# Perceiver layer on one core: context rows stationary in the weighted sum, the softmax division moved to the outputs, the context's scale folded into the key weights

## The chip, the cores and the metric

One core of a Trainium2 chip runs the whole program. The metric is the device time of one execution in microseconds. An execution has a profile, whose span runs from the first to the last instruction.

## The reference, cut to what matters

The layer is a cross attention, then a causal linear attention, then a two-of-eight expert layer, each added to its input. The change lies in the cross attention: 16 batches, 64 latents and 1024 context rows each, 16 heads of 64, all float32.

```python
lat = layer_norm(latents, ln_lat_g, ln_lat_b)
ctx = layer_norm(context, ln_ctx_g, ln_ctx_b)
q = (lat @ Wq)                      # 16 heads x 64
k, v = jnp.split(ctx @ Wkv, 2, axis=-1)
k = apply_rope(k, cos, sin)         # [x1*cos - x2*sin, x2*cos + x1*sin]
attn = jnp.clip(einsum('bhnd,bhsd->bhns', q, k) * scale, -11.0, 11.0)
attn = jax.nn.softmax(attn, axis=-1)
out = einsum('bhns,bhsd->bhnd', attn, v)
return out @ Wo + bo
```

The kernel never forms v: it takes the weighted sum of the normalised context rows first and multiplies by the value weights afterwards.

## The kernel before, in words

The order of the work is written out by hand. Each engine has a list of instructions and waits on counting semaphores. The cross attention has 128 steps (16 batches x 8 pairs of heads); in each, every engine runs its own function `step(j)`.

Float32 data that TensorE shall take in one pass is split in a high part, rounded to the fast format, and a low part, the rest; a product is then three matmuls (high x high, high x low, low x high).

In step j of the kernel before, in the order of their engine's list:

- TensorE (`step`, from L1321): the scores of pair j, 64 instructions on 64x64 corners of the array (L1332); the keys of pair j+2, twelve matmuls of 512 columns (L1346); two transposes of a normalised context tile (L1353); two transposes of the divided sum (L1362); the weighted sum of pair j-1, 24 matmuls that load the softmax weights and move 256 or 258 columns of context (L1380 to L1382); the value projection of pair j-2, 16 instructions on 64x64 corners (L1392).
- VectorE (`step`, from L912): centring of a context tile (L857), the output's sum (L844), the clamp of the exponentials (`clamped`, L863), scale and shift of the tile (L869), its moments (L877, L890), the keys times sine and cosine (L884, L895), the low part of the transposed tile (L902), and as the last large item the low part of the softmax weights (`weights_low`, L910); then the reciprocal of the denominators (L940), one element per partition.
- ScalarE (`step`, from L613): the exponential (L621), the high part of the context tile (L627), the division of the sum (L632), the high part of the softmax weights (`p_hi`, L637), and copies out of PSUM.
- GpSimd (`step`, from L498): waits for `ku_done`, `clamp_done` and the swapped keys, and adds the swapped product to the other (`kr`, L505), which finishes the rotary keys of the next step; the low part of a context tile (L509); and the reciprocal root of its variance (L513, L515).
- SyncE (`step`, from L360): four DMAs that swap the halves of `kw` across partitions into `ksw` (L368, SBUF to SBUF), a DMA that zeroes rows in DRAM for the expert layer (L371), and once in eight steps the next batch of context.

`pr`, the exponentials, has one buffer. The chain from one step to another is: keys, `kw`, swap DMA, add on GpSimd (`kr_done`), scores, exponential, clamp, high part, low part, weighted sum.

Of the kernel before, what the change touches and what calls it, by code (L numbers as in the profile page):

```python
# [34 lines left out]
STEPS = B * PAIRS  # L35
TILES = B * ST
# [21 lines left out]
def build(nc, x, ctx_1024, cos, sin, lat_g, lat_b, ctx_g, ctx_b, Wq, Wkv, Wo, bo, Wqkv, bqkv, Wout, bout, proj,  # L58
          Wg, W1, b1, W2, b2, out):
    with ExitStack() as ctx:  # L60
# [9 lines left out]
        vecs = sb("vecs", [P, 2, KC])  # L70
# [4 lines left out]
        rz = sb("rz", [P, 2])  # L75
# [3 lines left out]
        ctx_scale = sb("ctx_scale", [P, D])  # L79
        ctx_shift = sb("ctx_shift", [P, D])  # L80
# [6 lines left out]
        o_part = sb("o_part", [P, N])  # L87
# [13 lines left out]
        qs = sb("qs", [P, 2, PAIRS, N], F32, xattn)  # L101
        ct_hi = sb("ct_hi", [P, 2, KC, S], F32R, xattn)
        ct_lo = sb("ct_lo", [P, 2, KC, S], F32R, xattn)
        x_hi = sb("x_hi", [P, 2, ST, D + 2], F32R, xattn)
        x_lo = sb("x_lo", [P, 2, ST, D], F32R, xattn)
        with ExitStack() as first:
            vec_rows = sb("vec_rows", [2 * KC, P], F32, first)
            cs_raw = sb("cs_raw", [P, 2, ST, HALF], F32, first)
            crep = sb("crep", [P, 2, ST, P], F32, first)
# [6 lines left out]
            wk_raw = sb("wk_raw", [P, KC, INNER], F32, first)  # L116
            sb("between", [P, 7 * D], F32, first)
            wq_raw = sb("wq_raw", [P, KC, INNER], F32, first)
            latT = sb("latT", [P, KC, TOK], F32, first)
        zn = sb("zn", [P, D], F32, xattn)  # L120
        zts = sb("zts", [P, D], F32, xattn)
# [4 lines left out]
        p_hi = sb("p_hi", [P, 2, S], F32R, xattn)  # L126
        p_lo = sb("p_lo", [P, 2, S], F32R, xattn)
# [25 lines left out]
        bo_all = sb("bo_all", [P, D], F32, lin)  # L153
        bout_all = sb("bout_all", [P, D], F32, lin)
        xsT = sb("xsT", [P, 2, KC, ROWS], F32, lin)
        with ExitStack() as middle:
            wqkvT = sb("wqkvT", [P, KC, 3 * D], F32, middle)
            woutT = sb("woutT", [P, 2, D], F32, middle)
            feat_q = sb("feat_q", [P, 2, 4, 2, P], F32, middle)
        w2_lo_0 = sb("w2_lo_0", [P, FT, D], F32R, lin)  # L160
        w2_hi_0 = sb("w2_hi_0", [P, FT, D], F32R, lin)
        wo = sb("wo", [P, PAIRS, D], F32, lin)
        with ExitStack() as middle:
            feat_k = sb("feat_k", [P, 2, 4, 2, P], F32, middle)
            am = sb("am", [P, 2, 2, APAIRS, N], F32, middle)
        w2_hi_1 = sb("w2_hi_1", [P, FT, D], F32R, lin)
        w2_lo_1 = sb("w2_lo_1", [P, FT, D], F32R, lin)
# [22 lines left out]
        group_r = sb("group_r", [P, GT], F32, lin)  # L190
        group_at = sb("group_at", [P, GT], I32, lin)
# [20 lines left out]
        psZ, psT, psZT, psO = bank[:, 4], bank[:, 5], bank[:, 6], (bank[:, 7, 0:N], bank[:, 6, D:D + N])  # L212
        heads = bank[:, 2:4].rearrange("p h (t n) -> p h t n", n=N)
        pr_by_head = pr[:].rearrange("p (t h n) -> p h t n", h=2, n=N)


        wq_ld, wk_ld, wv_ld, wo_ld, cs_ld, vec_ld, affine_ld = (sem(n) for n in ("wq_ld", "wk_ld", "wv_ld", "wo_ld", "cs_ld", "vec_ld", "affine_ld"))
        x_ld = [sem(f"x_ld{i}") for i in range(2)]
        ctx_ld = [sem(f"ctx_ld{i}") for i in range(2)]
# [22 lines left out]
        pick_done, row_done, upto_done = sem("pick_done"), sem("row_done"), sem("upto_done")  # L242
# [8 lines left out]
        wk_hi_done, wk_lo_done, scaled = sem("wk_hi_done"), sem("wk_lo_done"), sem("scaled")  # L251
        crep_done, tab_ps, tab_done = sem("crep_done"), sem("tab_ps"), sem("tab_done")
        q_ps, q_act, q_dve = sem("q_ps"), sem("q_act"), sem("q_dve")
# [6 lines left out]
        qs_done = sem("qs_done")  # L260
        s_ps, exp_done, clamp_done, p_hi_done, p_lo_done = sem("s_ps"), sem("exp_done"), sem("clamp_done"), sem("p_hi_done"), sem("p_lo_done")
        z_ps, rz_done, zn_done, zt_ps, zts_done, o_ps, o_half, o_done = (
            sem(n) for n in ("z_ps", "rz_done", "zn_done", "zt_ps", "zts_done", "o_ps", "o_half", "o_done"))
# [11 lines left out]

        def expert_of(eng, g):

            return eng.value_load(group_expert[0:1, g:g + 1], min_val=0, max_val=E - 1)

        def place(j):  # L280

            return (j // PAIRS) % 2, j % PAIRS
# [17 lines left out]
        def wq_part(whole, n):  # L300

            return whole.rearrange("p t d -> p (t d)")[:, 0:KC * INNER].rearrange("p (k n) -> p k n", k=KC)[:, :, n * 2 * P:(n + 1) * 2 * P]

        def wq_high(n):

            return wq_part(x_hi[:, 1], n)

        def wq_low(n):

            return wq_part(x_lo[:, 1], n)  # L310

        def lat_part(part, u):

            return part[:, 1, :, S // 2 + u * P:S // 2 + (u + 1) * P]
# [12 lines left out]
        def _(sp):  # L327
            def ctx_rows(b):
                return ctx_1024[b].rearrange("(p t) d -> p t d", t=ST)
# [6 lines left out]
            for i, v in enumerate((lat_g, lat_b)):  # L336
# [3 lines left out]
            sp.dma_start(raw[:, 0], ctx_rows(0)).then_inc(ctx_ld[0], 16)  # L340
            sp.dma_start(ctx_scale[:], ctx_g.partition_broadcast(P)).then_inc(affine_ld, 16)
            sp.dma_start(ctx_shift[:], ctx_b.partition_broadcast(P)).then_inc(affine_ld, 16)
            sp.dma_start(wk_raw[:], kv[:, :, 0:INNER]).then_inc(wk_ld, 16)
            sp.dma_start(wv[:], kv[:, :, INNER:2 * INNER]).then_inc(wv_ld, 16)
            sp.wait_ge(latT_ps, TT)
            sp.dma_start(raw[:, 1], ctx_rows(1)).then_inc(ctx_ld[1], 16)
# [14 lines left out]
            def step(j):  # L361
                if there(j + 2):
                    i = j % 2

                    wait(sp, kw_done, j + 3)
# [3 lines left out]
                if j >= 0 and there(j):  # L369
                    o = j % 2 * N  # L370
                    sp.dma_start(x_slots[j * N:(j + 1) * N, :], fill[o:o + N, :]).then_inc(fill_st, 16)  # L371
                if j % PAIRS == 1 and there(j + 15):
                    p, n = j // PAIRS % 2, j // PAIRS + 2
                    wait(sp, xT_ps, ST * (n - 1))
                    wait(sp, x_lo_done, ST * (n - 1))
                    sp.dma_start(raw[:, p], ctx_rows(n)).then_inc(ctx_ld[p], 16)
# [3 lines left out]
            for j in range(STEPS):  # L380
                step(j)
                if j in (STEPS - 14, STEPS - 13):
                    half = slice((j - STEPS + 14) * TT // 2, (j - STEPS + 15) * TT // 2)
                    sp.wait_ge(x_lo_done, TILES - ST)
                    sp.wait_ge(xT_ps, TILES - ST)
                    sp.dma_start(raw[:, 0, half], x.rearrange("b n d -> (b n) d").rearrange("(t p) d -> p t d", p=P)[:, half]).then_inc(x2_ld, 16)
                if j in (STEPS - 10, STEPS - 9):
                    half = slice((j - STEPS + 10) * PAIRS // 2, (j - STEPS + 11) * PAIRS // 2)
                    sp.wait_ge(k_ps, STEPS - PAIRS)
                    sp.dma_start(wo[:, half], Wo.rearrange("(g p) n -> p g n", p=P)[:, half]).then_inc(wo_ld, 16)  # L390
                if j in (STEPS - 7, STEPS - 6):
                    i = j - STEPS + 7
                    sp.wait_ge(x_lo_done, TILES)
                    sp.wait_ge(xT_ps, TILES)
                    sp.dma_start(wqkv_raw[:, 3 * i:3 * i + 3], Wqkv.rearrange("(r p) c -> p r c", p=P)[:, 3 * i:3 * i + 3]).then_inc(wqkv_ld[i], 16)
                if j == STEPS - 5:
                    sp.wait_ge(s_ps, STEPS - PAIRS)
                    sp.dma_start(bo_all[:], bo.partition_broadcast(P)).then_inc(bo_ld, 16)
                    sp.dma_start(bout_all[:], bout.partition_broadcast(P)).then_inc(bo_ld, 16)
            sp.wait_ge(ku_done, STEPS)  # L400
            sp.dma_start(v_bias[:], bqkv[2 * D:3 * D].partition_broadcast(P)).then_inc(misc_ld, 16)
            sp.wait_ge(o_ps, STEPS)
# [8 lines left out]
            for e in range(0, E, 2):  # L411
                second_weights(e)
            for t in range(TT - 2):
# [47 lines left out]
        def _(pool):  # L461
# [36 lines left out]
            def step(j):  # L498
                if there(j + 1):
                    i = (j + 1) % 2  # L500
                    wait(pool, ku_done, j + 2)
                    if j > 0:
# [3 lines left out]
                if there(j + 7):  # L506
                    b, t = place(j + 7)
                    wait(pool, x_hi_done, j + 8)
                    pool.tensor_tensor(x_lo[:, b, t], raw[:, b, t], x_hi[:, b, t, 0:D].bitcast(F32), ALU.subtract).then_inc(x_lo_done, 1)  # L509
                if ST <= j + 12 and there(j + 12):  # L510
                    i = (j + 12) % 2
                    wait(pool, stats_done, j + 13)
                    pool.tensor_tensor(ve[:, i:i + 1], mv[:, i, 1:2], consts[:, 3:4], ALU.add).then_inc(var_done, 1)  # L513
                    wait(pool, var_done, j + 13)
                    pool.tensor_tensor(rstd[:, i:i + 1], ve[:, i:i + 1], consts[:, 2:3], ALU.pow).then_inc(rstd_done, 1)  # L515

# [18 lines left out]
            for j in range(-12, 0):  # L535
                step(j)
            for j in range(STEPS):
                step(j)
# [53 lines left out]
        def _(act):  # L592
# [5 lines left out]
            act.copy(vecs[:].rearrange("p v k -> p (v k)"), psZ[:, 0:2 * KC]).then_inc(vec_done, 1)  # L598

            def lat_turned(t):  # L600
                if t == 0:
                    act.wait_ge(vec_done, 1)
# [6 lines left out]
            def key_weights(k):  # L609
                act.wait_ge(wk_ld, 16)  # L610
                act.copy(wk_hi[:, k], wk_raw[:, k]).then_inc(wk_hi_done, 1)

            def step(j):  # L613
                if there(j - 3):
                    wait(act, o_ps, j - 2)
# [1126 lines left out]
```

## Time and profile before

| | us |
|---|---|
| median of three runs | 1293.83 (1292.77 to 1295.97) |
| span of the profiled execution | 1292.6 |
| its own time beyond the span | not listed; the runs lie 0.2 to 3.4 above the span |
| TensorE busy | 1269.5 |
| VectorE busy | 980.8 |
| ScalarE busy | 621.5 |
| GpSimd busy | 606.4 |

Matmuls overlap in their records, so TensorE's busy time is not its useful time. The distance between the starts of neighbouring instructions is what one costs. The attention's steady part is a step that repeats 128 times, between roughly 52 and 1020 us.

### The profile page before, as it was taken

What the parts mean: (1) busy time and instruction counts of PE and PEld (TensorE: products, weight loads), DVE (VectorE), ACT (ScalarE), POOL (GpSimd) and SP (SyncE); (2) the same over time, 40 slices, a digit from 0 to 9 for tenths busy, and PEclk for the clock granted to TensorE, in tenths of its full rate; (3) what the DMA queues carried; (4) which work ended last, traced back from release to release, by engine and by line L of the source; (5) the groups of instructions that cost most, each with busy time, mean ns of one, the idle gap of its engine ahead of it and who ended that gap; (6) DMA issues with size and microseconds to landing.
All of it is one profiled execution on the core that took longest, in us unless ns stands there. A gap on an engine that the chain in (4) does not pass through costs nothing.

```text
span 1292.6 us, 43933 instructions
## 1 busy us (share of the span) xinstructions
PE 1269.5 (98%) x18292; PEld 1136.7 (88%) x18292; DVE 980.8 (76%) x1973; ACT 621.5 (48%) x1264; POOL 606.4 (47%) x611
## 2 busy tenths in 40 slices
PE   7999999999999999999999999999999999999997
PEld 4788998899889889988999899889988878789997
DVE  7887787787778777877787777777766456668886
ACT  6344444444444454445444544454444333346664
POOL 3565554564455555545654555455443123323333
PEclk8999999999999999999999999999999999999999
DMA  6253343434343434343443434343454360556662
GB/s 221 62 122 88 95 116 85 108 75 121 80 108 77 121 79 108 80 117 82 106 114 88 108 76 116 87 108 75 112 122 108 79 228 31 179 174 189 187 189 82
DMA packets 71509, 145.56 MB, mean 113 GB/s; under 512 B 18248, under 2 KB 45584, under 8 KB 69136
## 3 DMA queue, kind: packets, MB, share of 16 engines
q1 hardware_dynamic: 67232, 138.53, 40.7%
q0 software_dynamic: 4080, 4.22, 1.6%
q8 instruction: 146, 2.39, 0.8%
q14 instruction: 51, 0.42, 0.1%
HBM read 61.74 MB, written 14.76 MB: 59 GB/s over the span
## 4 chain that ended last, share of the span: by engine, by line
PE 94%; DVE 1%; DMA 1%; ACT 1%; issue 1%; POOL 0%; SPq 0%; POOLq 0%; ACTq 0%; DVEq 0%
PE bank L1346 29%; PE bank L1380 10%; PE bank L1382 9%; PE bank L1381 9%; PE bank L1332 9%; PE bank L1646 6%; PE bank L1392 4%; PE bank L1362 2%; PE bank L1353 2%; PE bank L1477 2%; PE bank L1696 1%; PE bank L1698 1%; PE bank L1697 1%; PE bank L1503 1%; PE bank L1546 1%
## 5 line engine op out<-in xcount | busy, mean ns | idle before, releaser
L505 POOL TENSOR_TENSOR kr<-kr,ksw 128x1024 f32<-128x1024 f32 x128 | 318.5, 2488 | 449.4 <-DVE pr L863 345.7
L1380 PE MATMUL bank<-x_hi,p_hi 128*128 128x258 f32 x1024 | 300.9, 294 | 0.0
L1382 PE MATMUL bank<-x_hi,p_lo 128*128 128x258 f32 x1024 | 288.5, 282 | 0.0
L1381 PE MATMUL bank<-x_lo,p_hi 128*128 128x256 f32 x1024 | 287.8, 281 | 0.0
L1346 PE MATMUL bank<-ct_hi,wk_hi 128*128 128x512 f32 x512 | 213.5, 417 | 1.3 <-DVE kr L895 1.1
L884 DVE TENSOR_TENSOR kw<-bank,stab 128x1024 f32<-128x1024 f32 x128 | 156.7, 1224 | 61.0 <-PE bank L1346 60.9
L617 ACT COPY o_part<-bank 128x64 f32<-128x64 f32 x128 | 27.2, 213 | 362.5 <-PE bank L1392 362.5
L1346 PE MATMUL bank<-ct_hi,wk_lo 128*128 128x512 f32 x512 | 201.3, 393 | 0.0
L1346 PE MATMUL bank<-ct_lo,wk_hi 128*128 128x512 f32 x512 | 200.6, 392 | 0.0
L863 DVE TENSOR_SCALAR pr<-pr 128x1024 f32<-128x1024 f32 x128 | 90.1, 704 | 139.8 <-ACT pr L621 139.7
L1381 PEld LDWEIGHTS bank<-x_lo,p_hi 128*128 128x128 f32 x1024 | 194.7, 190 | 0.0
L1382 PEld LDWEIGHTS bank<-x_hi,p_lo 128*128 128x128 f32 x1024 | 193.6, 189 | 0.0
L1380 PEld LDWEIGHTS bank<-x_hi,p_hi 128*128 128x128 f32 x1024 | 193.2, 189 | 0.0
L621 ACT ACTIVATE pr<-bank 128x1024 f32<-128x1024 f32 x128 | 131.7, 1029 | 97.7 <-PE bank L1332 93.6
L910 DVE TENSOR_TENSOR p_lo<-pr,p_hi 128x1024 fp32r<-128x1024 f32 x128 | 158.4, 1237 | 2.2 <-ACT p_hi L637 2.2
L895 DVE TENSOR_TENSOR kr<-bank,ctab 128x1024 f32<-128x1024 f32 x128 | 152.8, 1194 | 0.0
L637 ACT CAST p_hi<-pr 128x1024 fp32r<-128x1024 f32 x128 | 134.7, 1052 | 17.1 <-DVE pr L863 6.3
L1332 PE MATMUL bank<-qs,kr 64*64 64x64 f32 x8192 | 142.6, 218 | 0.0
L1332 PEld LDWEIGHTS bank<-qs,kr 64*64 64x64 f32 x8192 | 131.8, 135 | 0.7 <-issue 0.5
L1346 PEld LDWEIGHTS bank<-ct_hi,wk_hi 128*128 128x128 f32 x512 | 95.9, 187 | 26.7 <-DVE kr L895 1.3
L1346 PEld LDWEIGHTS bank<-ct_hi,wk_lo 128*128 128x128 f32 x512 | 96.1, 188 | 21.0
L1346 PEld LDWEIGHTS bank<-ct_lo,wk_hi 128*128 128x128 f32 x512 | 96.3, 188 | 16.0
(220 smaller groups left out, 2180.8 us busy)
## 6 DMA issues: line engine op xcount, KB each, us to landing
ksw<-kw SPq DMA_DIRECT2D x512, 128.0 KB
raw<-in_ctx_dram SPq DMA_DIRECT2D x16, 1024.0 KB, 6.1
w_two<-in_L_ffn_W_dram SPq DMA_DIRECT2D x15, 1024.0 KB, 4.9
x_slots<-fill SPq DMA_DIRECT2D x128, 64.5 KB, 3.1
w_all<-in_L_ffn_W_dram SPq DMA_DIRECT2D x4, 2048.0 KB, 15.6
wo<-in_L_ffn_W_dram SPq DMA_DIRECT2D x7, 1024.0 KB, 5.0
xs<-x_slots SPq DMA_DIRECT2D x23, 129.0 KB, 2.2
raw<-in_x_dram SPq DMA_DIRECT2D x4, 512.0 KB, 4.6
```

What stands on the lines that cost most here:

```text
L505: pool.tensor_tensor(kr[:, i], kr[:, i], ksw[:, i], ALU.add).then_inc(kr_done, 1)
L621: act.activation(pr_by_head, heads, ACT.Exp, scale=SCALE).then_inc(exp_done, 1)
L637: act.copy(p_hi[:, i], pr[:]).then_inc(p_hi_done, 1)
L863: dve.tensor_scalar(pr[:], pr[:], LOW, HIGH, ALU.max, ALU.min).then_inc(clamp_done, 1)
L884: dve.tensor_tensor(kw[:, i], psK, stab[:], ALU.mult).then_inc(kw_done, 1)
L895: dve.tensor_tensor(kr[:, i], psK, ctab[:], ALU.mult).then_inc(ku_done, 1)
L910: dve.tensor_tensor(p_lo[:, i], pr[:], p_hi[:, i].bitcast(F32), ALU.subtract).then_inc(p_lo_done, 1)
L1332: last = pe.matmul(heads[c * N:(c + 1) * N, h, t], kr[rows, j % 2, at:at + N], qs[rows, b, g], start=True, stop=True)
L1346: last = pe.matmul(psK[:, cols], l[:, k, w], r[:, b, k, cols], start=(m == 0), stop=(m == len(parts) - 1))
L1380: pe.matmul(psZ[:, 0:D + 2], p_hi[:, i, c], x_hi[:, b, t], start=(t == 0), stop=False, skip_group_check=True)
L1381: pe.matmul(psZ[:, 0:D], p_hi[:, i, c], x_lo[:, b, t], start=False, stop=False, skip_group_check=True)
L1382: last = pe.matmul(psZ[:, 0:D + 2], p_lo[:, i, c], x_hi[:, b, t], start=False, stop=(t == ST - 1), skip_group_check=True)
```

## The change: what it does, and the diff

- The weighted sum is taken with the context rows as the loaded operand and the softmax weights of four pairs (512 columns) as the moving one. Per step it is twelve matmuls of 512 columns. Its result comes out transposed, so that the two transposes L1362 fall away.
- A step is now half the context rows for two pairs (before: all rows for one pair). Four steps (a quad) make four pairs. The value projection (`outputs`) runs once in four steps with four times the instructions.
- The softmax denominators are a row of the sum: the last context feature is replaced by ones, and the value weights are rewritten to suit (`value_weights`). Two DMAs per quad spread that row over partitions (`lsum`); VectorE takes the reciprocal of 256 columns and multiplies.
- The context's scale and shift are folded into the key weights, key biases and value weights. A context tile is normalised by one `tensor_scalar` (two instructions before). The rotary products take the bias in the same instruction, so they are `scalar_tensor_tensor` on 512 columns, four per step, where there were two `tensor_tensor` on 1024.
- VectorE's order in a step is new: tile work, clamp, `weights_low`, output, rotary products, low part of the tile. TensorE's is scores, sum of j-2, output, keys of j+2, transpose.
- The prologue gains eight bias matmuls and ten small DMAs for the biases; context tiles are prepared eight steps ahead (ten before), in three half-batch buffers.

The core of the diff:

```diff
 # VectorE
+            def outputs(j):
+                if due(j, 7):            # j = 7, 11, 15, ...
+                    n = (j - 7) // 4
+                    dve.wait_ge(o_half, n + 1)
+                    dve.tensor_tensor(o_part[:], psO[0], o_part[:], ALU.add).then_inc(o_sum, 1)
+                    dve.wait_ge(lsum_ld, 32 * (n + 1))
+                    dve.reciprocal(lsum[:], lsum[:]).then_inc(o_sum, 1)
+                    dve.wait_ge(o_sum, 2 * n + 2)
+                    dve.tensor_tensor(qo[...], o_part[...], lsum[...], ALU.mult).then_inc(o_done, 1)
+            def keys_turned(j):
...
+                    for a, g in enumerate(pairs_of(j + 2)):
+                        dve.wait_ge(k_ps, 2 * (j + 2) + a + 1)
...
+                        dve.scalar_tensor_tensor(out=kw[:, i, cols], in0=psK[:, cols], scalar=kbias[:, g:g + 1], in1=stab[:, places],
+                                                 op0=ALU.add, op1=ALU.mult).then_inc(kw_done, 1)
+                        dve.scalar_tensor_tensor(out=kr[:, i, cols], in0=psK[:, cols], scalar=kbias[:, g:g + 1], in1=ctab[:, places],
+                                                 op0=ALU.add, op1=ALU.mult).then_inc(ku_done, 1)
             def step(j):
...
+                normalised(j)
+                counted(j)
+                moments_taken(j)
+                clamped(j)
+                weights_low(j)
+                outputs(j)
+                keys_turned(j)
+                context_low(j)
 # GpSimd
             def step(j):
                 if there(j + 1):
                     i = (j + 1) % 2
-                    wait(pool, ku_done, j + 2)
-                    if j > 0:
+                    pool.wait_ge(ku_done, 2 * (j + 2))
+                    if j >= 0:
                         pool.wait_ge(clamp_done, j + 1)
                     pool.wait_ge(sw_ld[i], ((j + 1) // 2 + 1) * 64)
                     pool.tensor_tensor(kr[:, i], kr[:, i], ksw[:, i], ALU.add).then_inc(kr_done, 1)
 # SyncE
-                    wait(sp, kw_done, j + 3)
+                    sp.wait_ge(kw_done, 2 * (j + 3))
 # TensorE
+            def sums(j):
...
+                    pe.wait_ge(p_lo_done, 2 * h + 2)
...
+                    parts = [(t, l, r) for t in range(HT) for l, r in ((0, p_hi), (1, p_hi), (0, p_lo))]
+                    for m, (t, l, r) in enumerate(parts):
+                        last = pe.matmul(psZ[c], xc[:, slot_, l, t, cols], r[:, i, t], ...)
             def step(j):
+                scores(j)
+                sums(j - 2)
+                outputs(j)
+                keys(j + 2)
...
+                turn_context(j + 8)
```

## Rows read from the trace of the kernel before

**Rows 1.** The page's busy times: us, share of the span, instructions.
```profile
PE 1269.5 (98%) x18292; PEld 1136.7 (88%) x18292; DVE 980.8 (76%) x1973; ACT 621.5 (48%) x1264; POOL 606.4 (47%) x611
```
**Rows 2.** Busy time by stretch, attention's second half; last columns: clock, DMA share, GB/s.
```profile
520.00:970.00 450.00, 450.00 (x7131) 404.85 (x7121) 347.20 (x638) 214.63 (x416) 230.31 (x226) 1.00 0.41 99
```
**Rows 3.** The critical chain in order of time, one step: start, us, what.
```profile
610.65 0.93 PE bank L1332 x64
611.59 2.96 PE bank L1346 x12
614.54 0.22 PE bank L1353 x2
614.76 0.22 PE bank L1362 x2
614.98 0.12 PE bank L1380
...
617.86 0.39 PE bank L1392 x16
```
**Rows 4.** Timeline of a step, scores to high part: start, us, engine, instruction.
```profile
602.87 1.11 PE L1332 MATMUL bank<-qs,kr 64*64 64x64 f32 x64
...
605.11 0.69 DVE L863 TENSOR_SCALAR pr<-pr 128x1024 f32<-128x1024 f32 x1 [1.23 <-ACT pr L621]
...
605.84 1.05 ACT L637 CAST p_hi<-pr 128x1024 fp32r<-128x1024 f32 x1
```
**Rows 5.** VectorE's groups by line and shape: busy us, mean ns, idle before.
```profile
L910 DVE TENSOR_TENSOR p_lo<-pr,p_hi 128x1024 fp32r<-128x1024 f32 x128 | 158.4, 1237 | 2.2 <-ACT p_hi L637 2.2
L884 DVE TENSOR_TENSOR kw<-bank,stab 128x1024 f32<-128x1024 f32 x128 | 156.7, 1224 | 61.0 <-PE bank L1346 60.9
L857 DVE SCALAR_TENSOR_TENSOR raw<-raw,mv,ctx_scale 128x256 f32<-128x256 f32 x120 | 57.7, 481 | 12.0 <-POOL rstd L515 11.8
L902 DVE TENSOR_TENSOR ct_lo<-bank,ct_hi 128x256 fp32r<-128x256 f32 x128 | 52.8, 413 | 1.9 <-ACT ct_hi L643 1.8
L877 DVE BATCH_NORM_STATS2 bst<-raw 128x6 f32<-128x256 f32 x120 | 50.5, 421 | 0.0
L890 DVE BATCH_NORM_AGGREGATE mv<-bst 128x2 f32<-128x6 f32 x120 | 20.8, 173 | 0.1
L1001 DVE TENSOR_SCALAR xn<-raw,mom,rsd 128x256 f32<-128x256 f32 x8 | 3.3, 414 | 0.0
L1032 DVE RECIPROCAL rec<-rec 128x16 f32<-128x16 f32 x8 | 2.0, 253 | 0.3
L940 DVE RECIPROCAL rz<-bank 128x1 f32<-128x1 f32 x128 | 20.3, 159 | 4.9 <-PE bank L1382 4.9
```
**Rows 6.** Timeline: two places where `p_lo` and GpSimd run at once.
```profile
1007.46 2.36 POOL L505 TENSOR_TENSOR kr<-kr,ksw 128x1024 f32<-128x1024 f32 x1 [5.20 <-DVE pr L863]
1008.44 2.46 DVE L910 TENSOR_TENSOR p_lo<-pr,p_hi 128x1024 fp32r<-128x1024 f32 x1 [1.11 <-ACT p_hi L637]
...
609.65 1.22 DVE L910 TENSOR_TENSOR p_lo<-pr,p_hi 128x1024 fp32r<-128x1024 f32 x1
609.73 1.54 POOL L515 TENSOR_TENSOR rstd<-ve,consts 128x1 f32<-128x1 f32 x1
```
**Rows 7.** The swap: its issue and the add it releases (timeline).
```profile
570.36 2.41 SPq L368 DMA_DIRECT2D ksw<-kw  x4
...
615.83 2.41 SPq L368 DMA_DIRECT2D ksw<-kw  x4
...
622.01 2.40 POOL L505 TENSOR_TENSOR kr<-kr,ksw 128x1024 f32<-128x1024 f32 x1 [2.83 <-DMA ksw<-kw]
```
**Rows 8.** Busy time by stretch, as rows 2: DMA share after the swap at 570.36.
```profile
574.40:574.80 0.40, 0.40 (x3) 0.33 (x2) 0.00 (x0) 0.40 (x2) 0.00 (x0) 1.00 0.06 16
```
**Rows 9.** Who waited for whom: us in total, times, longest.
```profile
POOL kr L505 <- DVE pr L863: 345.7, 96, 5.2
POOL kr L505 <- DMA ksw<-kw: 103.7, 31, 5.8
```

More of the change, by code:

```diff
@@ L534, in _ @@
             constants()
-            for j in range(-12, 0):
-                step(j)
-            for j in range(STEPS):
+            for j in range(-5, STEPS):
                 step(j)
@@ new lines, in step @@
+                if there(j):
+                    act.wait_ge(clamp_done, j + 1)
+                    wait(act, z_ps, j // 2 * 2 - 2)
+                    act.copy(step_part(p_hi, j), pr_parts).then_inc(p_hi_done, 1)
+                if there(j + 5):
+                    n, t = tile_at(j + 5)
+                    act.wait_ge(xhat_done, j + 6)
+                    if t == 0 and j + 5 >= 3 * HT:
+                        h = (j + 5) // HT - 3
+                        act.wait_ge(z_ps, h // 2 * PAIRS + h % 2 * 2 + 6)
+                    act.copy(xc[:, n, 0, t, 0:D - 1], raw[:, (j + 5) // ST % 2, (j + 5) % ST, 0:D - 1]).then_inc(x_hi_done, 1)
@@ new lines, in value_weights, with normalised @@
+            def value_weights(k):
+                rows = slice(0, P if k == 0 else P - 1)
+                dve.scalar_tensor_tensor(out=wv[rows, k], in0=wv[rows, k], scalar=vecs[rows, 2, k:k + 1], in1=w_last[rows, :],
+                                         op0=ALU.mult, op1=ALU.subtract).then_inc(wv_done, 1)
+            def normalised(j):
+                if there(j + 9):
+                    n = j + 9
+                    dve.wait_ge(rstd_done, n + 1)
+                    mean, scale = (xl_mom[:, n, 0:1], xl_rsd[:, n:n + 1]) if n < ST else (mv[:, n % 2, 0:1], rstd[:, n % 2:n % 2 + 1])
+                    x_ = raw[:, n // ST % 2, n % ST]
+                    dve.tensor_scalar(x_, x_, mean, scale, ALU.subtract, ALU.mult).then_inc(xhat_done, 1)
@@ new lines, in keys @@
+            def keys(j):
+                if there(j):
+                    h = half_of(j)
+                    for a, g in enumerate(pairs_of(j)):
+                        w = slice(g * P, (g + 1) * P)
+                        wait(pe, ku_done, 2 * (j - 1) + a + 1)
+                        if a == 0:
+                            pe.wait_ge(ct_lo_done, HT * (h + 1))
+                        parts = [(l, r, k) for k in range(KC) for l, r in ((wk_hi, 0), (wk_hi, 1), (wk_lo, 0))]
+                        for m, (l, r, k) in enumerate(parts):
+                            last = pe.matmul(psK[:, a * 512:(a + 1) * 512], l[:, k, w], ct[:, h % 3, r, k], start=(m == 0), stop=(m == len(parts) - 1))
+                        last.then_inc(k_ps, 1)
@@ L1487, in turn @@
                 last.then_inc(xnT_ps, 1)
-            for j in range(STEPS + 2):
+            for j in range(2, STEPS):
                 step(j)
-                if j == STEPS:
-                    turn(0)
+            step(STEPS)
+            turn(0)
+            step(STEPS + 1)
+            project_heads(2, 0, 2)
+            outputs(STEPS + 3)
             project_heads(2, 2, 4)
```

718 lines of the change are left out of this document (358 added, 360 removed).

## The prediction

> **What bounds the kernel now.** I read the page's busy times, then busy time by stretch, then the chain, then the timeline of one step. [...] The chain in order of time holds nothing but TensorE: scores 0.93, keys 2.96, two pairs of transposes 0.22 each, the sum from 614.98 to 617.86, which is 2.88, and the value projection 0.39 [rows 3]. Together 7.60 us, and 128 such steps are three quarters of the time. VectorE is busy 347.2 of 450 us, which is 5.86 of each 7.60 [rows 2]. The means of its eleven instructions in a step sum to about 6.7 (seven of them or their twins stand in [rows 5]), so neighbours overlap in the records by some 0.08; I take that off where nothing is waited for.
>
> So the change has to be read twice: what it takes from TensorE's 7.60, and what it does to the other engines' loops, which have had 1.7 us of slack.
>
> **TensorE.** The transposes L1362 go: 0.22. The sum becomes twelve matmuls of 512 columns, the form of the keys: 2.96 with the ramp at its start, instead of 2.88, so the larger loaded operand brings nothing. The keys now follow it directly, without their ramp: 2.96 less 0.2. The projection is 64 instructions in one of four steps; at the scores' rate that is 0.93 with 0.2 for the switches, or 0.29 a step against 0.39. New step: 0.93 + 2.96 + 2.76 + 0.22 + 0.29 = 7.16, say 7.2. If TensorE stayed the bound, 0.4 us a step would be gained.
>
> **VectorE's line.** Its order is clamp, then at once `p_lo`, which waits for ScalarE's `p_hi`. Before, tile work and the rotary products filled that wait; now nothing does. From the start of a clamp, with [rows 4]: clamp 0.69, 0.04, `p_hi` 1.05, 0.04, `p_lo` 1.24 [rows 5]: it ends at 3.06. Then the rotary products. A `scalar_tensor_tensor` of 256 elements takes 0.48; from 256 to 1024 elements a `tensor_tensor` grows from 0.413 to 1.224, 1.06 ns an element [rows 5]; so one of 512 is 0.48 + 0.27 = 0.75, with overlap 0.67, four times 2.68, against 2.42 for the two before. Bounds: 0.68 (a plain product of that size) to 0.80. Then the tile's low part 0.33, the next tile's normalisation 0.33 (0.41 in L1001 [rows 5], instead of two at 0.48), moments 0.42 and 0.17 with a wait between. That is 3.06 - 0.08 + 2.68 + 0.33 + 0.33 + 0.61 = 6.93, and clamp again. The exponential hides in it.
>
> One step in four adds the output: sum 0.33, reciprocal of 256, product 0.42. The trace has reciprocals of one element (0.159) and of sixteen (0.253) [rows 5]: 6.3 ns an element more, which makes 1.76 us for 256. [...] I take 1.76, the slope of the nearest rows: 2.5 us per quad, 0.63 a step. The 128 small reciprocals L940 and half the tile's affine work are already out of this line. It comes to 7.56 a step.
>
> [...]
>
> **Where `p_lo` meets GpSimd's add.** GpSimd's `kr` add (2.4 us) is released by the clamp. Before, `p_lo` came four microseconds after the clamp, behind the rotary products, when the add was over. Now it comes 1.13 us after the clamp's end, in the middle of the add. One step near the end of the attention, where the products had run out, shows what that costs: add 1007.46 to 1009.82, `p_lo` started 1008.44 and took 2.46 instead of 1.24, ending 1.08 after the add [rows 6]. The other way round `rstd` began while `p_lo` ran, took 1.54, and ended 0.40 after it [rows 6]. The two exclude each other, whoever starts first.
>
> [...]
>
> So there are two kinds of step.
> - Add first, starting g after the clamp's start (at least 0.8): `p_lo` ends at g + 2.4 + 1.08, the rest of VectorE's line is 3.9: the step is g + 7.35.
> - `p_lo` first: it ends at 3.06, the add 2.3 later, scores start 0.1 later, and from scores to clamp it is 2.24, 602.87 to 605.11 [rows 4]: 7.7.
>
> Neither is below 7.60; that is the core of the forecast.
>
> **Which kind, by the swap.** The add also needs the swapped keys. The last `kw` ends at 5.05 in a `p_lo`-first step. From the issue of four swaps at 570.36 [rows 7] the DMA queues are nearly empty 4.0 us later, with the row-zeroing write behind them [rows 8]; so a good swap takes about 3.9. A late one took 622.01 - 615.83 = 6.2 [rows 7], and 31 of 127 adds were released by the swap, that is by one above 5.3 [rows 9]. Before, 5.3 us passed anyway until the clamp. After a 7.7 step the good swap is there at 5.05 + 3.9 - 7.7 = 1.25: add first, g 1.25, a step of 8.6. In that one `kw` ends at 6.75, and the next add is ready at 6.75 + 3.9 - 8.6 = 2.05, after `p_lo` has begun at 1.8: 7.7 again. They alternate; a late swap puts the add behind `p_lo`. I take two thirds at 7.7 and one third at 8.6: 8.0. The quad's 2.5 us count in full in an add-first step and 6.93 + 2.5 - 7.7 = 1.7 in the other, 2.1 on the mean, 0.5 a step.
>
> **Sum.** 8.0 + 0.5 = 8.5 against 7.60: 0.9 us more. About 125 of the 128 steps have both products and the add: +112 us. Ends: the prologue gets ten small DMAs for the biases at some 0.6 us each on SyncE's queue (2.41 for four [rows 7]) before the first rotary product, less two steps of tile preparation; the tail waits for the `lsum` DMA and the reciprocal, less one transposition. Each between -5 and +10, taken as nothing. ScalarE loses the division and two copies and has slack. 1292.6 + 112 = 1404.6 of the profiled execution; the median of the runs is 1.2 above its span: 1406.
>
> **Rivals.**
> - Slower, by the swap alone: kw at 5.05, swap L, add 2.4, scores to clamp 2.24 and 0.15 of handing over make a ring of 9.84 + L over two steps, and 2.5 in one of the two rings' four: (2 (9.84 + L) + 2.5) / 4. With L 3.9 it is 7.5, below the forecast; with 6.2 all along it is 8.65: +131, 1425. For it: the late swaps come in runs of steps. Against: three in four are in time. 0.17.
> - Faster: TensorE keeps the bound at 7.2, 0.4 x 125 = -50: 1244. It needs `p_lo` to pass beside the add, and VectorE's quad work under about 1.1 us, that is a reciprocal of some 0.4. Up to there the gain on TensorE stands; above 7.6 on VectorE's line it is a loss. For it: TensorE is the whole chain now. Against: rows 6 and the reciprocals' slope. 0.08.
> - No change to speak of: the exclusion seldom bites and swaps come in 3.6, so VectorE's 7.56 sets the step: -5, 1289. 0.07.
> - The forecast 0.68.
>
> **Range.** Lowest of the forecast's own case: always `p_lo` first, reciprocal 0.42, (3 x 7.7 + 8.1) / 4 = 7.8, +25: 1319. Highest: 7.7 and 9.1 in turn, the quad in full and a reciprocal of 2.3: 9.1, +187: 1481. I cut both: 1330 to 1460. A change under 0.3% (4 us) can't be told from none in this kernel. Faster: 0.08 and half of the 0.07, 0.11; same 0.04; slower 0.85.
>
> **What would show it.** Right: TensorE below 90% busy in the steady stretch with waits on GpSimd's add; `p_lo` with a mean well above 1.24, in two clusters (1.2 and 2 to 3.5 us), or adds that start inside it and take over 3; VectorE in the chain; the reciprocal near 1.8; the idle time ahead of the add put down to the swap DMA. TensorE's sum should be twelve matmuls about 0.23 apart. Wrong: `p_lo` at 1.24 while an add runs, or TensorE at 100% again. [...]

## The result, and the profile of the changed kernel

The changed kernel takes 1433.67 us (median of four runs, 1424.90 to 1434.21) against 1293.39 for the kernel before beside it: a ratio of 1.107 (95% interval 1.104 to 1.110). The forecast was 1406 in a range of 1330 to 1460. Sign and size came out; the share that each cause has in it did not, as the experiments show. The runs of each kernel lie within 1.1% of one another but for one: of the five of the kernel with the division one step later, one took 1374.49 at a mean granted clock of 0.847, and the ratio given there leaves it out.

The busy times of the changed kernel answer to [rows 1]: TensorE has fallen from 98% of the span to 90%, though it is busy longer.

```profile
PE 1285.4 (90%) x16516; PEld 1059.8 (74%) x16516; DVE 1082.1 (76%) x1924; ACT 559.5 (39%) x983; POOL 612.8 (43%) x611
```

Busy time by stretch, as [rows 2] (TensorE, weight loads, VectorE, ScalarE, GpSimd; then clock, DMA share, GB/s): 44 of 450 us TensorE stands still (in [rows 2] none), and its granted clock is 0.96, no longer 1.00.

```profile
520.00:970.00 450.00, 405.64 (x5596) 327.75 (x5595) 359.60 (x568) 163.56 (x251) 212.59 (x212) 0.96 0.47 91
```

The groups by line: busy us, mean ns of one, idle before and its releaser. What matters in them: GpSimd waits 558.7 us ahead of the add until the swap has landed (in [rows 9] it was 103.7); TensorE waits 119 us for the add; the reciprocal takes 1744 ns; and `p_lo`, at 1399 ns on the mean, is far nearer to the 1225 that it takes undisturbed than the forecast had it.

```profile
L562 POOL TENSOR_TENSOR kr<-kr,ksw 128x1024 f32<-128x1024 f32 x128 | 322.1, 2517 | 580.8 <-DMA ksw<-kw 558.7
L962 DVE TENSOR_TENSOR p_lo<-pr,p_hi 128x1024 fp32r<-128x1024 f32 x128 | 179.1, 1399 | 142.9 <-ACT p_hi L689 135.1
L1376 PE MATMUL bank<-qo,kr 64*64 64x64 f32 x8192 | 156.6, 228 | 119.3 <-POOL kr L562 119.0
L972 DVE SCALAR_TENSOR_TENSOR kw<-bank,kbias,stab 128x512 f32<-128x512 f32 x256 | 190.6, 745 | 28.8 <-PE bank L1390 27.4
L925 DVE TENSOR_SCALAR raw<-raw,mv,rstd 128x256 f32<-128x256 f32 x120 | 72.5, 604 | 20.5 <-POOL rstd L568 18.8
L953 DVE RECIPROCAL lsum<-lsum 128x256 f32<-128x256 f32 x32 | 55.8, 1744 | 4.4 <-DMA lsum<-zt 4.4
```

The critical chain in order of time (start, us, what), from an add to the one two steps later, and on to the one after the next two. It answers to [rows 3], where TensorE alone stood.

```profile
595.64 2.64 POOL kr L562
...
598.33 1.16 PE bank L1376 x64
599.49 2.95 PE bank L1420 x12
602.44 1.14 PE bank L1445 x64
...
603.60 0.38 ACT o_part L701
...
604.00 0.42 DVE o_part L951
604.43 1.67 DVE lsum L953
...
606.47 0.74 DVE kw L972
607.21 0.66 DVE kr L974
607.87 0.67 DVE kw L972
...
608.56 0.51 SPq L422
...
610.38 2.37 DMA ksw<-kw
...
612.90 2.63 POOL kr L562
...
615.58 1.16 PE bank L1376 x64
616.74 4.54 PE bank L1420 x12
621.28 1.40 PE bank L1390 x6
...
622.70 0.75 DVE kw L972
...
626.88 2.32 DMA ksw<-kw
...
629.36 2.49 POOL kr L562
```

Read it as a ring over two steps. The add releases the scores; behind them in TensorE's order stands the whole sum (L1420) and only then the projection (L1445) and the keys (L1390); VectorE's products follow, then the swap, then the add. The first ring, with the quad's division in it, takes 612.90 - 595.64 = 17.26 us, the second 16.46: 33.7 over four steps, 8.43 a step. From the 20th to the 116th clamp the mean step is 8.55; by its place among the four of a quad it is 7.89, 8.41, 7.86 and 10.03, where the kernel before had 7.59 throughout.

In the second ring the twelve matmuls of the sum take 4.54 instead of 2.95. Busy time by stretch at that place: TensorE had worked 0.42 of the 2.30 us from 613.30, and the clock then stood at 0.55 on the mean. Inside that stretch, from 618.00 to 620.00, it is 0.50, called its lower level from here on, and from one of these matmuls to the next it is 0.43 us, against 0.23 at 1.00.

```profile
613.30:615.60 2.30, 0.42 (x7) 0.16 (x5) 2.30 (x5) 0.37 (x1) 2.30 (x2) 1.00 0.00 0
...
617.50:620.80 3.30, 3.30 (x10) 2.57 (x9) 2.01 (x3) 2.16 (x4) 0.00 (x0) 0.55 0.50 111
621.00:623.00 2.00, 2.00 (x11) 1.62 (x10) 0.30 (x1) 0.00 (x0) 1.92 (x1) 1.00 0.65 164
```

From 150 to 1050 us the clock was at its lower level for 71.7 of 900 us, and for none in the kernel before. From the 20th to the 116th clamp, TensorE's pieces of the critical chain lie at the lower level for 56 us. An estimate from that and from the 0.43 and 0.23: half of it, 28 us or 0.29 a step, is what the clock costs, unless another wait would come in its place.

The spans differ by 138.6 us (1292.6 and 1431.2). Of these the first clamp starts 9.0 later (62.93 against 53.94), the 127 steps take 123.9 more, and the part behind the start of the last clamp 5.7 more.

### The profile page after: what moved, and what is told of

It reads as the page before. It is cut to its first block, busy times and chain, and to the rows that moved or that the text cites. A ratio compares the mean times of both kernels' runs of the same rounds, so it can differ in the third digit from the quotient of the medians.

```text
span 1431.2 us, 39843 instructions
## 1 busy us (share of the span) xinstructions
PE 1285.4 (90%) x16516; PEld 1059.8 (74%) x16516; DVE 1082.1 (76%) x1924; ACT 559.5 (39%) x983; POOL 612.8 (43%) x611
## 4 chain that ended last, share of the span: by engine, by line
PE 41%; DVE 16%; DMA 13%; POOL 11%; SPq 9%; issue 6%; ACT 3%; POOLq 0%; ACTq 0%; DVEq 0%
PE bank L1420 14%; POOL kr L562 11%; DMA ksw<-kw 11%; SPq L422 8%; DVE kw L972 6%; PE bank L1376 6%; PE bank L1729 5%; DVE lsum L953 3%; PE bank L1390 3%; DVE kr L974 3%; PE bank L1445 2%; PE bank L1557 2%; PE bank L1779 1%; PE bank L1781 1%; PE bank L1780 1%
## 5 line engine op out<-in xcount | busy, mean ns | idle before, releaser
L562 POOL TENSOR_TENSOR kr<-kr,ksw 128x1024 f32<-128x1024 f32 x128 | 322.1, 2517 | 580.8 <-DMA ksw<-kw 558.7
L1420 PE MATMUL bank<-p_hi,xc 128*128 128x512 f32 x1024 | 356.5, 431 | 0.0
L1390 PE MATMUL bank<-ct,wk_hi 128*128 128x512 f32 x1024 | 320.5, 394 | 1.8 <-DVE kr L974 1.8
L962 DVE TENSOR_TENSOR p_lo<-pr,p_hi 128x1024 fp32r<-128x1024 f32 x128 | 179.1, 1399 | 142.9 <-ACT p_hi L689 135.1
L1376 PE MATMUL bank<-qo,kr 64*64 64x64 f32 x8192 | 156.6, 228 | 119.3 <-POOL kr L562 119.0
L1376 PEld LDWEIGHTS bank<-qo,kr 64*64 64x64 f32 x8192 | 138.4, 141 | 147.1 <-POOL kr L562 131.5
L1420 PEld LDWEIGHTS bank<-p_hi,xc 128*128 128x128 f32 x1024 | 198.5, 204 | 47.0
L1390 PEld LDWEIGHTS bank<-ct,wk_hi 128*128 128x128 f32 x1024 | 190.1, 188 | 43.0 <-DVE kr L974 2.2
L972 DVE SCALAR_TENSOR_TENSOR kw<-bank,kbias,stab 128x512 f32<-128x512 f32 x256 | 190.6, 745 | 28.8 <-PE bank L1390 27.4
L1420 PE MATMUL bank<-p_lo,xc 128*128 128x512 f32 x512 | 211.5, 413 | 0.0
L1390 PE MATMUL bank<-ct,wk_lo 128*128 128x512 f32 x512 | 201.3, 393 | 0.0
L974 DVE SCALAR_TENSOR_TENSOR kr<-bank,kbias,ctab 128x512 f32<-128x512 f32 x256 | 189.7, 741 | 0.0
L689 ACT CAST p_hi<-pr 128x1024 fp32r<-128x1024 f32 x128 | 134.4, 1050 | 126.2 <-DVE pr L944 126.2
L1420 PEld LDWEIGHTS bank<-p_lo,xc 128*128 128x128 f32 x512 | 104.0, 203 | 24.6
L1390 PEld LDWEIGHTS bank<-ct,wk_lo 128*128 128x128 f32 x512 | 96.4, 188 | 20.5
L572 POOL TENSOR_TENSOR xc<-raw,xc 128x255 fp32r<-128x255 f32 x128 | 95.5, 746 | 12.7 <-ACT xc L696 12.7
L925 DVE TENSOR_SCALAR raw<-raw,mv,rstd 128x256 f32<-128x256 f32 x120 | 72.5, 604 | 20.5 <-POOL rstd L568 18.8
```

The costliest lines, as they stand in the source:

```text
L562: pool.tensor_tensor(kr[:, i], kr[:, i], ksw[:, i], ALU.add).then_inc(kr_done, 1)
L572: pool.tensor_tensor(xc[:, n, 1, t, 0:D - 1], raw[:, (j + 5) // ST % 2, (j + 5) % ST, 0:D - 1], xc[:, n, 0, t, 0:D - 1].bitcast(F32), ALU. ...
L689: act.copy(step_part(p_hi, j), pr_parts).then_inc(p_hi_done, 1)
L962: dve.tensor_tensor(step_part(p_lo, j), pr_parts, step_part(p_hi, j).bitcast(F32), ALU.subtract).then_inc(p_lo_done, 1)
L972: dve.scalar_tensor_tensor(out=kw[:, i, cols], in0=psK[:, cols], scalar=kbias[:, g:g + 1], in1=stab[:, places], op0=ALU.add, op1=ALU.mult) ...
L974: dve.scalar_tensor_tensor(out=kr[:, i, cols], in0=psK[:, cols], scalar=kbias[:, g:g + 1], in1=ctab[:, places], op0=ALU.add, op1=ALU.mult) ...
```

## The experiments

The mean step is that from the 20th to the 116th clamp of the profiled execution; "kinds" are the four lengths of a step by its place in a quad, the fourth holding the division. The kernel before ran at 1292.69 to 1293.08 beside these.

**Without the swap.** Is it the exclusion (`p_lo` and the add can't run at once) or the swap?

```diff
-                    for r in range(4):
-                        sp.dma_start(ksw[...], kw[...]).then_inc(sw_ld[i], 16)
-                    pool.wait_ge(sw_ld[i], ...)
-                    pool.tensor_tensor(kr[:, i], kr[:, i], ksw[:, i], ALU.add)
+                    pool.wait_ge(kw_done, 2 * (j + 2))
+                    pool.tensor_tensor(kr[:, i], kr[:, i], kw[:, i], ALU.add)
```

> The changed kernel without the swap DMAs: the four DMAs of a step are left out and GpSimd adds kw itself instead of ksw, so the rotary keys are not the reference's. Swap theory (the ring kw, swap, add, scores, clamp sets the step, nothing else matters much): the ring loses 5.1 of its 15 us, VectorE's own line of 7.56 is left, about 1300 us. Exclusion theory (p_lo and the add can't run at once): the add now starts 0.8 after every clamp, p_lo is held in nearly every step (mean 2.4 instead of 1.4), step 0.8 + 7.35 + 0.63 = 8.8, about 1460 us: taking the DMA away gains nothing or makes it slower.

Measured 1429.53 us, ratio 1.106 (1.104 to 1.108); kinds 8.02, 8.01, 8.01, 10.50. The swap, on the chain of the changed kernel in the rows above, is gone, and 4 us are gained. The timeline (start, us, engine, instruction, idle before and releaser) shows what came in its place: the add starts with the clamp's end, `p_lo` falls into it, and 127 of 128 take 2.47.

```profile
609.85 2.38 POOL L559 TENSOR_TENSOR kr<-kr,kw 128x1024 f32<-128x1024 f32 x1 [5.63 <-DVE pr L941]
610.83 2.48 DVE L959 TENSOR_TENSOR p_lo<-pr,p_hi 128x1024 fp32r<-128x1024 f32 x1 [1.11 <-ACT p_hi L686]
```

The step is then VectorE's own line and the delay: 6.76 (next run) + 1.25 = 8.01. The forecast's mechanism is real, but it sets the pace only here, where the swap no longer delays the add.

**Without swap and without add.** The add shrinks to one column (and the swapped product is left out).

```diff
-                    pool.tensor_tensor(kr[:, i], kr[:, i], kw[:, i], ALU.add)
+                    pool.tensor_tensor(kr[:, i, 0:1], kr[:, i, 0:1], kw[:, i, 0:1], ALU.add)
```

> The changed kernel without the swap DMAs and with an add of one column instead of 1024 (the rotary keys lack their second product). Without the swap alone it stayed at 1429.5 with p_lo at 2.47 in all steps. Exclusion theory: p_lo back at 1.24, VectorE's own line of 6.93 and 2.5 in one of four is left: 7.5 to 7.6, 1295 to 1310. If p_lo is slow for another reason (its new access pattern of 128 columns in turn), p_lo stays near 2.4 and the time above 1400.

Measured 1269.27, ratio 0.982 (0.980 to 0.984); kinds 6.76, 6.76, 6.76, 9.21. Every `p_lo` takes 1.23. This is VectorE's line without anything else: the forecast had 6.93 and 2.5 for a quad, the chip 6.76 and 2.45. So VectorE's work alone would have allowed less than the kernel before, and less than the 1295 to 1310 expected. TensorE stood still for only 1.2 of 450 us in the stretch of [rows 2], so its own pace lies just below this one.

**Without the swap, the add behind `p_lo`.** Neither swap nor exclusion. Beside the edits of the run without the swap:

```diff
-                        pool.wait_ge(clamp_done, j + 1)
+                        pool.wait_ge(p_lo_done, j + 1)
```

> Left out: the four swap DMAs (the add takes the product that was not exchanged), as in the run without swap, which took 1429.53 us with every p_lo held by the add (2.47 us). Here the add waits for p_lo instead of the clamp, so that neither holds the other. By the prediction's formula the round is then clamp, p_hi, p_lo of 1.22, add of 2.4, scores and exp one behind the other: 7.7 in three kinds of step and some 9.5 in the fourth, mean 8.15, 1365 to 1375 us. If the exclusion of the two was the cause of the whole loss, it would fall to TensorE's pace, 7.3 to 7.6 a step, 1270 to 1300 us. If the loss lay in the quad's work and VectorE's order, no gain: 1420 to 1435.

Measured 1417.71, ratio 1.096 (1.094 to 1.099): both causes are out, and 16 us come back, not the 60 or more that the formula gave. Kinds 7.88, 8.67, 7.86, 9.71. Its chain again runs over two steps:

```profile
604.48 2.36 POOL kr L559
...
606.88 1.16 PE bank L1373 x64
608.04 4.55 PE bank L1417 x12
612.59 1.40 PE bank L1387 x6
...
614.01 0.75 DVE kw L969
...
617.91 0.67 DVE pr L941
...
618.61 1.06 ACT p_hi L686
...
619.69 1.24 DVE p_lo L959
...
621.05 2.39 POOL kr L559
```

The way back is through the clamp instead of the swap, but the first half is the same: add, scores, the whole sum, keys, products. The two-step rings of this one run 604.48 to 621.05 and on to 638.60: 34.1 for four steps. The clock is at its lower level for 88.7 of 900 us here, once in every quad. On the chain the sum then takes 4.3 to 4.55 instead of 2.95, up to 1.6 us a quad or 0.4 a step: an estimate without it is 8.13, the mean that had been expected (8.15), though from a ring over one step and not over two.

So three limits of nearly one length, 8.43 to 8.63 a step, come up in turn: the ring by the swap, VectorE's line with a held `p_lo`, and the ring by clamp and `p_lo`. The first and the last have 0.4 of the lower clock in them in the rows shown, the second none. Whoever takes one away finds the next. The next runs change what the two rings share, the order.

**VectorE's order alone: products before `p_lo`.**

```diff
                 clamped(j)
+                keys_turned(j)
                 weights_low(j)
                 outputs(j)
-                keys_turned(j)
```

> The changed kernel with VectorE's order clamp, rotary products, p_lo, output, low tile part; TensorE's order stays (sum ahead of keys). Exclusion theory: p_lo comes when the add is over, VectorE's line falls to 6.93 - 1.1 + 0.6 = 6.4, TensorE's 7.2 would be left, 1250. Swap theory: kw now waits for the keys, which come 4 to 5 us after the scores' start behind the sum; scores to last kw 7.5, swap 5.1, add and hand-over 2.65: 15.3 over two steps and the value projection in one of four, about 7.9, 1330 to 1340. In both p_lo is back at 1.24.

Measured 1468.28, ratio 1.136 (1.131 to 1.140), slower still; kinds 8.97, 7.58, 8.12, 11.06. A miss. `p_lo` is free (1.30), but now it stands behind products that wait for the keys, which stand behind the sum in TensorE's order: of the idle time ahead of the products 289.9 us are put down to the keys. And ScalarE's next exponential waits for `p_lo` (176.6 us), since `pr` has one buffer.

**TensorE's order alone: keys before the sum.**

```diff
                 scores(j)
-                sums(j - 2)
-                outputs(j)
                 keys(j + 2)
+                outputs(j)
+                sums(j - 2)
```

> The changed kernel with TensorE's order scores, keys, output, sum; VectorE's order stays (p_lo directly behind the clamp). Both theories: kw stands behind p_lo on VectorE and not behind the keys, so little moves, 8.4 to 8.6 a step, 1405 to 1435; only the 27 us in which kw waited for the keys can go. A TensorE-order theory (the sum ahead of the keys is the whole loss) expects about 1260.

Measured 1489.74, ratio 1.152 (1.150 to 1.155); kinds 8.69, 8.12, 7.91, 11.54. Another miss: the keys come early, but VectorE still takes `p_lo` first, and in the fourth step ScalarE's half of the output stands behind a copy (L696) that waits for the sum just moved back.

**Both orders.**

> Both orders at once: VectorE clamp, rotary products, p_lo, output; TensorE scores, keys, output, sum. Swap theory: scores to last kw 5.0, swap 5.1, add 2.65: 12.8 over two steps, 6.4, below TensorE's 7.2, which then bounds: 1240 to 1265. Exclusion theory: the same, p_lo free. If the larger loaded operand or the clock cost TensorE time, it stays above 1293.

Measured 1334.69, ratio 1.033 (1.031 to 1.034), 99 us less than the changed kernel, where each of its halves alone had cost 35 and 56. Kinds 7.23, 7.01, 6.97, 9.89. In three of four steps the chain is TensorE again:

```profile
604.79 0.22 PE bank L1400 x2
605.01 1.09 PE bank L1376 x64
606.10 2.95 PE bank L1390 x12
609.04 2.73 PE bank L1420 x12
...
620.47 0.37 ACT o_part L701
...
620.87 0.42 DVE o_part L951
621.29 1.67 DVE lsum L953
...
622.99 0.43 DVE qo L955
623.41 0.34 DVE ct L982
...
623.89 2.98 PE bank L1390 x12
```

0.22 + 1.09 + 2.95 + 2.73 = 6.99, and a quarter of the projection's 1.09 makes 7.3, near the 7.2 of the forecast. The expected 1240 to 1265 did not come: the fourth step is 2.9 longer. The projection takes 1.3 of it, its ramps included. For the rest TensorE stands still twice in such a step, 1.37 us in which the transposes wait for the output's sum (L951), and 0.95 in which the keys wait for the tile's low part (L982), which stands behind the division.

**The division last.** With both orders, ScalarE copies its half of the output ahead of the context tile, and reciprocal and product stand behind `context_low`.

```diff
                 clamped(j)
+                keys_turned(j)
                 weights_low(j)
                 outputs(j)
-                keys_turned(j)
                 context_low(j)
+                divided(j)
```

`outputs` keeps the sum of the halves, `divided` has the reciprocal and the product.

> The kernel with both orders and two more moves: ScalarE copies the output's half before the context tile, and VectorE divides after the low part of the transposed tile, so that the keys of the next half don't wait for the reciprocal. The ring of output, reciprocal, low tile part, keys made one step in four 9.9 us there and the other three 7.0. If that ring is the rest of the loss, the fourth step falls to 7.0 + 1.2 for the value projection, 7.3 on the mean: 1260 to 1275, the first of these kernels faster than before. If the swap DMA or the exclusion is the rest, the fourth step stays above 9 and the time at 1320 to 1335.

Measured 1317.80, ratio 1.020 (1.018 to 1.021); kinds 6.24, 7.12, 6.83, 10.35. The step after the fourth got 1.0 shorter, the fourth 0.5 longer. The swap is late there (from the last `kw` to the add 7.0 us on the mean, against 5.1 and 5.7 in two of the others), and 58 of 128 `p_lo` are held by the add.

**The division one step later.** With both orders and ScalarE's earlier copy, as before.

```diff
                 clamped(j)
+                keys_turned(j)
+                outputs(j)
                 weights_low(j)
-                outputs(j)
-                keys_turned(j)
+                divided(j - 1)
                 context_low(j)
```

> The version with both new orders (VectorE turns the keys before the low part of the weights, TensorE computes keys before outputs and sums), and with the quad's work spread: ScalarE copies the half of the outputs right behind p_hi, VectorE adds the other half before p_lo, and the reciprocal and the product stand one step later, behind that step's p_lo. It ran at 7.63 a step with everything in one step (6.24, 7.12, 6.83, 10.35). If the tenth step's length is the 2.6 us of VectorE work at one place, spreading it over two steps gives VectorE's own line, 7.2 to 7.4 a step, 1268 to 1290 us, faster than the kernel before. If the add's exclusion (p_lo 1.75 instead of 1.23 there) and the swap fill the room, 7.6 a step remain, 1310 to 1325 us.

Measured 1281.77 (median of five), ratio 0.991 (0.990 to 0.993): 152 us less than the changed kernel, and 0.9% less than the kernel before. Kinds 7.71, 6.28, 7.08, 8.34, mean 7.35, as expected of spread work. Busy time by stretch, as [rows 2]: TensorE stands still for 1.8 of 450 us.

```profile
520.00:970.00 450.00, 448.24 (x6516) 364.74 (x6515) 426.94 (x644) 187.87 (x289) 282.92 (x235) 1.00 0.55 106
```

Of its `p_lo`, 52 of 128 are still held by the add (the mean of all is 1.71), and that costs next to nothing, for TensorE is the bound again. From scores to scores it takes 6.99 us in three steps and 8.31 in the fourth, 7.32 on the mean. The forecast's rival with TensorE at 7.2 was to give 50 us; the 127 steps give 26.9 (961.0 to 934.1), and the ends take back 11.7 (7.8 ahead of the first clamp, 3.8 behind the last). With both orders and the division's place mended, the change is good for 11 us.

**The reciprocal, twice.** First a plain copy of 256 columns in its place, `dve.tensor_copy(lsum[:], lsum[:])`.

> The changed kernel with a copy in place of the reciprocal (the outputs are multiplied by the denominators instead of divided). The reciprocal takes 1.74, a copy of 256 columns 0.3 to 0.4. The swap ring and VectorE's line both hold the quad's work in one step of four, so that step falls from 10.0 to 8.6 or 8.7: 0.34 a step on the mean, 42 us, 1385 to 1400. If TensorE or its clock set that step, nothing changes.

Measured 1429.73, ratio 1.106. It is inconclusive, for the copy took 1.38 us on the mean, since 28 of 32 met the add (one at 603.25 took 2.06). Then a copy of one column, `dve.tensor_copy(lsum[:, 0:1], lsum[:, 0:1])`.

> Left out: the reciprocal; a copy of one column stands in its place, so the outputs are multiplied by the denominators themselves. In the earlier run with a copy of 256 columns that copy took 1.38 us, since it met the add as well, and nothing could be told. Here some 1.65 us of VectorE work go from one step in four. If the reciprocal lies on the path of the output step (the fourth kind of step, 10.03 us in the changed kernel): that step 8.4 to 8.7, the others as they are, mean step 8.2, 1383 to 1392 us. If the swap and the exclusion set that step and the reciprocal lies beside them: the step stays at 9.5 to 10, and the time within 10 us of 1433.

Measured 1407.17 (1399.85 and 1414.50), ratio 1.088 (1.083 to 1.094); kinds 8.20, 8.15, 7.75, 9.59. 26 us come back of the 53 that 32 chain pieces of 1.67 make. That lies between the two expectations: the division is on the ring, but about half of it only takes the place of a wait for something else. The share isn't exact, for the two runs differ by 15 us and in their mean granted clock (0.981 and 0.967).

**The order alone, in the kernel before.** `weights_low` directly behind the clamp, everything else as it was.

```diff
                     clamped(j)
+                    weights_low(j)
                     shifted(j)
...
                     context_low(j)
-                    weights_low(j)
```

> The kernel before the change, with one line moved: VectorE takes the low part of the softmax weights directly behind the clamp, as the changed kernel does. Exclusion theory: steps with the add first take 0.8 + 3.5 and 4.0 for the rest of its line, 8.3, those with p_lo first 7.7; so 7.7 to 8.3 against 7.59: 1305 to 1380. If the order does no harm by itself, TensorE keeps the bound: 1293.

Measured 1464.54, ratio 1.134 (1.131 to 1.136), a step of 9.02: 171 us for one line moved, more than the whole change costs and far above what was expected. 124 of 127 adds are now released by the swap (448 us), where [rows 9] had 31. But the swap has only 4.8 us of the critical chain between 200 and 1000 us. Most of it is VectorE's, and nearly a quarter (24.6%) is one instruction, the scale and shift of a context tile (L869), which reads two inputs in SBUF. Its group here and in the kernel before:

```profile
L869 DVE SCALAR_TENSOR_TENSOR raw<-raw,rstd,ctx_shift 128x256 f32<-128x256 f32 x120 | 264.9, 2207 | 0.1
...
L869 DVE SCALAR_TENSOR_TENSOR raw<-raw,rstd,ctx_shift 128x256 f32<-128x256 f32 x120 | 57.5, 479 | 0.1
```

In the kernel before it started ahead of the add and took 0.48 every time. Behind `p_lo` it starts inside the add in 93 of 128 steps, takes 2.59 or more there and ends 0.28 after it. `p_lo` itself is held in only 13. The timeline shows both, the common case and, further up, the rare one:

```profile
610.91 2.88 DVE L910 TENSOR_TENSOR p_lo<-pr,p_hi 128x1024 fp32r<-128x1024 f32 x1 [1.12 <-ACT p_hi L637]
612.65 1.63 POOL L509 TENSOR_TENSOR x_lo<-raw,x_hi 128x256 fp32r<-128x256 f32 x1
...
620.20 1.23 DVE L910 TENSOR_TENSOR p_lo<-pr,p_hi 128x1024 fp32r<-128x1024 f32 x1 [1.11 <-ACT p_hi L637]
620.34 3.33 POOL L505 TENSOR_TENSOR kr<-kr,ksw 128x1024 f32<-128x1024 f32 x1 [3.33 <-DMA ksw<-kw]
...
621.34 2.61 DVE L869 SCALAR_TENSOR_TENSOR raw<-raw,rstd,ctx_shift 128x256 f32<-128x256 f32 x1
```

So the exclusion has its price here, some 200 us of VectorE's time (93 times 2.14), but on an instruction that the changed kernel no longer has. The 171 us are not what this order costs there.

## Why the prediction came out, and where its steps failed

- **TensorE 7.2 a step:** right within 0.2. 7.32 where it never waits (the division one step later). The scores take 1.09 where 0.93 was taken, keys and sum together 5.68 against 5.72.
- **VectorE 6.93, and 2.5 per quad:** right within 0.2; 6.76 and 2.45 where nothing else held it.
- **Reciprocal 1.76 us:** 1.744, so the 6.3 ns an element read from two small ones held up to 256. The 0.42 and 2.3 that the range takes for it are shown by no run: all 32 in the changed kernel took 1.74 or 1.75. A product of 512 columns: 0.745 and 0.741 against 0.75.
- **`p_lo` and the add exclude each other:** right as behaviour, in every overlap of more than 0.1 us of the two in every trace. In the changed kernel a `p_lo` that started in the add ended 1.08 or 1.09 us after it, and an add that started in `p_lo` ended 2.20 to 2.29 after that. The products, which have one input in PSUM, were not held: 189 ran wholly inside an add of the changed kernel and took 0.745 on the mean, the 323 others 0.742; in the kernel before, 126 did and took 1.224, the four that met no add 1.214. Wrong as the main price in this kernel: 14 of 128 `p_lo` were held, 22 us of duration above 1.23 in all. The other way round, 69 adds started inside a `p_lo`, and the 128 adds took 0.13 us longer on the mean than without the swap, 17 us.
- **The step that failed: "Which kind, by the swap".** The prediction took 3.9 us from the last `kw` to the add, and had the swap ring lead back to `kw` by exponential, clamp and `p_lo`. Measured, the swap takes 5.1 (median; 4.33 at least: four issues behind one another and then 2.3 to 2.4 of transfer), so the alternation of two kinds of step never arose: 121 of 127 adds wait for the swap. And the ring closes by TensorE: add 2.64, scores 1.16, sum 2.95, then projection and division (4.0) or keys (1.40), three products 2.1, swap 4.4. The prediction had written that the keys follow the sum, but only as a saved ramp of 0.2; the wait of VectorE's products for them was not in any of its formulas.
- **The rival "by the swap alone"** had the right releaser and 1425 us, but for a wrong ring and a swap of 6.2. With the median of 5.1 its formula gives 8.1 a step, the chip 8.55.
- **The clock** has no term in the sum of the prediction. It fell in pieces, 71.7 of 900 us. Where it lay on the chain it cost 4.54 - 2.95 = 1.6 us a time. By the estimate from the chain it cost up to 28 us over 96 steps, 0.29 of the 0.96 a step that were lost. No run takes the clock away by itself: the one without the swap had no lower clock between 150 and 1050 us and was hardly faster, but there another limit, the held `p_lo`, had come in.
- **Ends of zero:** they cost 9.0 and 5.7, together a tenth of the loss.
- **The signs named:** the add's idle time is put down to the swap, and the reciprocal is there. `p_lo` has its two clusters, but with only 14 in the upper one; 5 adds took over 3 us; TensorE is at 90.1% of the steady stretch, where "below 90%" was named.

So 8.5 a step was forecast and 8.55 came. That the number fits so well is luck: the ring that set it was not the one forecast, and it reached that length only with the lower clock in it (33.7 less 1.6 over four steps is an estimated 8.0). That the exclusion gives 8.63 once the swap is gone is shown. That it was the main cause in the changed kernel is refuted by that kernel's own trace (14 held of 128), and the run with the add behind `p_lo` has 8.53 with neither, 0.4 of it by the clock. That the pair of orders was the main cause is shown by the run with both mended, 99 us of the 140.

## What to carry to other kernels

Write the ring out over as many steps as the buffers allow and through the order of every engine, what stands between two of its links included. Here the main fault lay in a pair of orders, and each half mended alone made it worse. Where taking one wait away brings nothing, look for a second ring of the same length and change what the two share. After a move, look for every instruction whose duration changed: a held one showed no wait here, and the chain charged it to its own engine (L869 in the kernel before with `p_lo` moved: 2207 ns with 0.1 us idle before all 120, and 24.6% of the chain). Work that comes once in four steps is spread over its neighbours, not placed at one point: that was worth 36 us here (1317.80 to 1281.77) between two kernels that differ only in where VectorE does the quad's work.

## What the runs showed of the hardware

- The exclusion goes further than `p_lo`. The tile's scale and shift with two inputs in SBUF (L869) took 0.48 free and 2.6 where it started inside an add. The tile's normalisation (L925), a `tensor_scalar` with two operands of one column, took 0.40 or 0.41 in the 64 cases that met nothing on GpSimd, and in the 63 that met the low part of a context tile (L572) 0.81 in 48 and 0.62 to 0.80 in the rest; its mean is 604 ns in the changed kernel and 399 without the swap. A copy of 256 columns within SBUF took 1.38 on the mean in the place of the reciprocal, and 0.29 in the four cases that met nothing on GpSimd. The reciprocal of the same columns met the add in 30 of 32 cases and took 1.74 or 1.75 in all.
- In the changed kernel the granted clock fell for 3.4 us after TensorE had stood still for 1.9 of 2.3 us (row 613.30 above), and was back by itself. In the run with the add behind `p_lo` it fell after a pause of 2.2 us ahead of 606.88 and stayed at 1.00 after one of 0.9 ahead of 623.49. Without the swap TensorE waited for the add in 90 of 128 steps, 90.5 us in all and never over 1.7 at a time between 150 and 1000 us, and the clock stayed up there. In the run with both orders it fell twice between 150 and 1050 us, at the second of a pair of pauses of 1.37 and 0.95, and not at the other such pairs.
- Another instruction on GpSimd that meets `p_lo` is lengthened as well: `x_lo` of 0.74 took 1.63 in the kernel before with `p_lo` moved.
- In the kernel before, a matmul of 512 columns on unsplit float32 (L1412) starts 0.43 us after the one before it, one on the high and low parts (L1346) 0.23.
